# Context split once into fp16 parts, x2 written to a doubled buffer, and a new order of all engines, in a two-layer attention and expert kernel

## What is computed

```
x = x + autocorrelation(layernorm(x), ctx)     # per column: correlate over the 128 rows,
                                               # top 9 lags, softmax, sum of shifted ctx
x = x + experts0(layernorm(x))                 # xf @ W_base.T + b_base
                                               #   + top 2 of 8 experts, rank 16
x = x + window_attention(layernorm(x), ctx)    # rows are channels: q = Wq x, k = Wk ctx, v = Wv ctx,
                                               # 8 heads of 16, window of 16 columns, then Wo
x = x + experts1(layernorm(x))                 # top 2 of 4 experts, rank 16
```

## Time and profile before

| | us |
|---|---|
| median of three runs | 2023.16 (2018.21 to 2026.01) |
| profiled execution, its own time | 2025.97 |
| its span | 2024.1 |
| PE busy | 1855.6 (92%) |
| DVE busy | 1519.6 (75%) |
| ACT busy | 1347.2 (67%) |
| POOL busy | 1088.4 (54%) |
| mean granted clock of TensorE | 0.969 |

### The profile page before, as it was taken

The page is one execution under the profiler, slowest core; times in us unless marked ns, Lnnn a source line. Parts: engine busy times, 40 slices in busy tenths (PEclk is TensorE's granted clock), DMA queues, the critical chain, the costliest instruction groups (busy, mean ns, idle before and its releaser), DMA issues. The chain is left out here.

```text
span 2024.1 us, 49212 instructions
## 1 busy us (share of the span) xinstructions
PE 1855.6 (92%) x18912; PEld 1131.0 (56%) x18912; DVE 1519.6 (75%) x4529; ACT 1347.2 (67%) x1958; POOL 1088.4 (54%) x902
## 2 busy tenths in 40 slices
PE   4889999999999999999999999999999999999975
PEld 2355555665555655555565655566555565655543
DVE  6677777778777778777877777777777877877743
ACT  4267776677776677776667777667777666777652
POOL 2565555466555466555556655546655645655541
PEclk8899999999999999999999999999999999999985
DMA  5001110011111011111001111001111110111000
GB/s 217 22 33 53 52 52 31 31 52 41 52 52 36 27 50 41 52 52 52 31 31 43 50 52 52 31 31 49 45 52 52 44 39 31 41 52 42 21 6 17
DMA packets 25165, 91.56 MB, mean 45 GB/s; under 512 B 3184, under 2 KB 3312, under 8 KB 24624
## 3 DMA queue, kind: packets, MB, share of 16 engines
q1 hardware_dynamic: 25136, 91.17, 12.8%
HBM read 74.39 MB, written 16.78 MB: 45 GB/s over the span
## 5 line engine op out<-in xcount | busy, mean ns | idle before, releaser
L548 PE MATMUL pb<-w_base_h,even_words 128*128 128x512 f16 x1024 | 324.8, 379 | 0.4 <-ACT mid_t L851 0.4
L1370 POOL TENSOR_TENSOR p_hl<-sc,p_hl 128x512 f16<-128x512 f32 x128 | 178.1, 1391 | 180.3 <-ACT p_hl L730 180.3
L450 PE MATMUL pa<-ctx_a,tab 128*128 128x512 f32 x384 | 203.4, 655 | 35.6 <-ACT q_spec L730 24.3
L840 ACT ACTIVATE q_diag<-sc,par 32x1024 f32<-32x1024 f32 x192 | 216.1, 1141 | 19.9 <-DVE sc L1100 17.5
L1413 POOL TENSOR_TENSOR sc<-sc,sc_rec 128x512 f32<-128x512 f32 x128 | 134.2, 1048 | 146.8 <-DVE sc_rec L1176 146.8
L548 PE MATMUL pb<-w_base_l,even_words 128*128 128x512 f16 x512 | 193.9, 379 | 0.0
L617 PEld LDWEIGHTS pc<-sc_t,v_diag 128*128 128x128 f16 x6144 | 173.8, 97 | 32.9 <-issue 23.8
L450 PE MATMUL pa<-xn_a,tab 128*128 128x512 f32 x384 | 186.3, 609 | 1.5 <-ACT xn_a L730 1.5
L617 PE MATMUL pc<-sc_t,v_diag 128*128 128x32 f16 x6144 | 173.9, 177 | 6.5 <-ACT rows_c L730 6.5
L594 PE MATMUL pc<-k_h,q_diag 128*128 128x32 f16 x2048 | 169.1, 177 | 0.0
L595 PE MATMUL pc<-k_l,q_diag 128*128 128x32 f16 x2048 | 168.5, 177 | 0.0
(11 more groups left out here) (149 smaller groups left out, 5068.5 us busy)
## 6 DMA issues: line engine op xcount, KB each, us to landing
x_a<-in_x SPq DMA_DIRECT2D x32, 512.0 KB, 3.3
ctx_a<-in_ctx_in SPq DMA_DIRECT2D x32, 512.0 KB, 3.2
x_res<-in_x SPq DMA_DIRECT2D x32, 512.0 KB, 3.9
ctx_b<-in_ctx_in SPq DMA_DIRECT2D x32, 512.0 KB, 4.0
out<-rows_c SPq DMA_DIRECT2D x32, 512.0 KB, 2.9
v_diag<-in_base_w SPq DMA_DIRECT2D x4, 1024.0 KB, 10.1
tab<-in_spectra SPq DMA_DIRECT2D x1, 576.0 KB, 5.2
q_diag<-in_ra SPq DMA_DIRECT2D x1, 544.0 KB, 13.8
```

What stands on the lines that cost most here:

```text
L450: last = mm(place[:, n + h, :], lhsT, moving[:, h * HALF:(h + 1) * HALF], start=True, stop=True)
L548: mm(pb[:, h, :], rows[:, cols], weights[:, j, h * HALF:(h + 1) * HALF], start=(j == 0 and m == 0), stop=False)
L840: nc.scalar.activation(q_diag[rows, :, col:col + QB], source, ACT.Copy, scale=par[rows, a:a + 1]).then_inc(qd_out.sem, 1)
L1370: g_.tensor_tensor(part[:, :, :, LO], sc[:, g % 2, :, :], part[:, :, :, HI], ALU.subtract)\
```

## The change

1. **Context split once.** ctx is loaded once a batch (before: twice). ACT makes its high fp16 part (`ctx_high`), POOL the low one (`ctx_low`), in one of two slots of `ctx_hl`. The tables FWD, CTX_RE, CTX_IM and the weights Wk, Wv are split likewise at the start, and `project_ctx` makes each of the five context products from three fp16 products. ctx in float32 shares its buffer with `x_res`.
2. **Experts in fp16 parts.** The gates' result `mid` is split on DVE (two instructions more in `gates`), its transposes and the products in `b_base_end` and `c_delta` are fp16: six and four products of 128x512. `w_b0` and `w_b1` are split at the start.
3. **x2 straight to `x_c`**, which now has two slots; `b_move` on POOL is gone.
4. **Query product from PSUM.** `q_spec` and its copy are gone, DVE computes both c1 and c2 from `pa`. `a_values` is two copies of 64 rows and one of 128 (before: four of 64), with signs moved into the tables CORR_1 and CORR_2.
5. **Keys and values into `pa`**, before x2 is there (before: into `pb`, after x2).
6. `q_diag` is filled by halves of its blocks (twelve copies of 32x512 on ACT, four on POOL); the scores' first two groups need the first half only. `c_result` is in halves.
7. **All batches written out**, without a loop, in a new order on all engines. A step now begins in the middle of what was one: `live(k)` says whether batch i-k is there.

```diff
+            def project_ctx(n, slot, table):
+
+                high, low = ctx_hl[:, slot, 0, :], ctx_hl[:, slot, 1, :]
+                for h in range(2):
+                    cols = slice(h * HALF, (h + 1) * HALF)
+                    mm(pa[:, n + h, :], w_ctx_h[:, table, :], high[:, cols], start=True, stop=False)
+                    mm(pa[:, n + h, :], w_ctx_h[:, table, :], low[:, cols], start=False, stop=False)
+                    last = mm(pa[:, n + h, :], w_ctx_l[:, table, :], high[:, cols], start=False, stop=True)
+                return last
+
...
                 for h in range(2):
-                    last = mm(pb[:, h, :], mid_t[0][:, :], w_b0[:, h * HALF:(h + 1) * HALF],
-                              start=False, stop=True)
+                    cols = slice(h * HALF, (h + 1) * HALF)
+                    mm(pb[:, h, :], mid0_t[:, 0, :], w_b0_h[:, cols], start=False, stop=False)
+                    mm(pb[:, h, :], mid0_t[:, 0, :], w_b0_l[:, cols], start=False, stop=False)
+                    last = mm(pb[:, h, :], mid0_t[:, 1, :], w_b0_h[:, cols], start=False, stop=True)
                 last.then_inc(mm_ffn[0].sem, 1)
...
             def b_mid(b):
-                pe.wait_ge(mid_out[0].sem, mid_out[0].after(b))
-                nc.tensor.transpose(pb[:, 0, MID_AT:MID_AT + P], mid[0][:, :], ident[:, :])\
+                pe.wait_ge(midl_out[0].sem, midl_out[0].after(b))
+                nc.tensor.transpose(mid0_place[:, 0:P], mid_hl[0][:, 0, :], ident_h[:, :])
+                nc.tensor.transpose(mid0_place[:, P:2 * P], mid_hl[0][:, 1, :], ident_h[:, :])\
                     .then_inc(tr_mid[0].sem, 1)
...
-            def b_keys(b):
-                pe.wait_ge(ctxb_in.sem, ctxb_in.after(b))
-                pe.wait_ge(x2_out.sem, x2_out.after(b))
-                project(pb, 0, ctx_b, w_att[:, 1, :]).then_inc(mm_k.sem, 1)
-
-            def b_values(b):
+            def b_keys(b, slot):
+                if last_a(b):
+                    pe.wait_ge(prod_w.sem, prod_w.after(b))
+                else:
+                    pe.wait_ge(vagg_out.sem, vagg_out.after(b + 1))
+                project_ctx(2, slot, CTX_K).then_inc(mm_k.sem, 1)
+
+            def b_values(b, slot):
                 pe.wait_ge(kl_out.sem, kl_out.after(b))
-                project(pb, 0, ctx_b, w_att[:, 2, :]).then_inc(mm_v.sem, 1)
+                project_ctx(2, slot, CTX_V).then_inc(mm_v.sem, 1)
...
                 for h in range(2):
-                    last = mm(pc[:, h, :], mid_t[1][:, :], w_b1[:, h * HALF:(h + 1) * HALF],
-                              start=True, stop=True)
+                    cols = slice(h * HALF, (h + 1) * HALF)
+                    mm(pc[:, h, :], mid1_t[:, :], w_b1_hh[:, cols], start=True, stop=False)
+                    last = mm(pc[:, h, :], mid1_t[:, :], w_b1_l0[:, cols], start=False, stop=True)
                 last.then_inc(mm_ffn[1].sem, 1)
...
+            def step(i, odd, live):
+                if live(2):
+                    b_router(i - 2)
+                if live(3):
+                    c_attend(i - 3, 0)
+                if live(2):
+                    b_keys(i - 2, odd)
+                    b_base(i - 2, 1, 0)
+                if live(3):
+                    c_scores(i - 3, 3)
+                if live(2):
+                    b_base(i - 2, 1, 1)
+                    b_mid(i - 2)
+                if live(3):
+                    c_attend(i - 3, 1)
+                if live(2):
+                    b_values(i - 2, odd)
+                    b_base(i - 2, 0, 0)
+                if live(3):
+                    c_attend(i - 3, 2)
+                if live(2):
+                    b_base(i - 2, 0, 1)
+                if live(3):
+                    c_attend(i - 3, 3)
+                if live(2):
+                    b_base_end(i - 2)
+                if live(1):
+                    a_transpose(i - 1)
+                if live(3):
+                    c_output(i - 3)
+                if live(1):
+                    a_weights(i - 1, 1)
+                    a_weights(i - 1, 0)
+                if live(2):
+                    b_queries(i - 2)
+                if live(3):
+                    rows_to_features(i - 3, 1, 3, xn_c, pc)
+                    c_router(i - 3)
+                if live(1):
+                    a_aggregate(i - 1, 0)
+                    a_aggregate(i - 1, 1)
+                if live(3):
+                    c_mid(i - 3)
+                    c_delta(i - 3)
+                if live(0):
+                    a_context(i, odd)
+                if live(2):
+                    c_scores(i - 2, 0)
+                if live(0):
                     a_query(i)
-                if do_c:
-                    c_scores(c, 1)
-                if do_b:
...
+            def ctx_high(b, slot):
+
+                act.wait_ge(ctx_read.sem, ctx_read.after(b))
+                if not early(b):
+                    act.wait_ge(mm_k.sem, mm_k.after(b - 2))
+                    act.wait_ge(mm_v.sem, mm_v.after(b - 2))
+                copy(ctx_hl[:, slot, 0, :], ctx_f[:, :]).then_inc(ctxh_out.sem, 1)
+
+            def a_values(b):
+
+                act.wait_ge(mm_ctx.sem, mm_ctx.after(b))
+                if not first(b):
+                    act.wait_ge(sum_w.sem, sum_w.after(b - 1, 1))
+                for half in range(2):
+                    rows = slice(half * P // 2, (half + 1) * P // 2)
+                    other = slice((1 - half) * P // 2, (2 - half) * P // 2)
+                    copy(v_im[rows, :], pa_lo[other, :]).then_inc(v_out.sem, 1)
+                if not first(b):
+                    act.wait_ge(sum_w.sem, sum_w.after(b - 1))
+                copy(v_re[:, :], pa_lo).then_inc(v_out.sem, 1)
...
-                        act.wait_ge(mm_sc.sem, mm_sc.after(b - 1))
+                        act.wait_ge(mm_sc.sem, mm_sc.after(b - 1, 2 * half + 2))
                 rows = slice(32 * pair, 32 * pair + 32)
-                source = q_hl[rows, :].rearrange("p (n t) -> p n t", t=QB)
+                blocks = slice(half * NBLK // 2, (half + 1) * NBLK // 2)
+                source = q_hl[rows, :].rearrange("p (n t) -> p n t", t=QB)[:, blocks]
                 col = (2 * pair + a) * QB
-                nc.scalar.activation(q_diag[rows, :, col:col + QB], source, ACT.Copy,
+                nc.scalar.activation(q_diag[rows, blocks, col:col + QB], source, ACT.Copy,
                                      scale=par[rows, a:a + 1]).then_inc(qd_out.sem, 1)
 
...
             def a_product(b):
-                dve.wait_ge(q_out.sem, q_out.after(b))
+                if first(b):
+                    tables_ready()
+                dve.wait_ge(mm_q.sem, mm_q.after(b))
                 dve.wait_ge(v_out.sem, v_out.after(b, 2))
-                v.tensor_tensor(c1[:, :], q_spec[:, :], v_re[:, :], ALU.mult).then_inc(prod_q.sem, 1)
+                if not first(b):
+                    dve.wait_ge(mm_agg.sem, mm_agg.after(b - 1))
+                v.tensor_tensor(c2, pa_hi, v_im[:, :], ALU.mult).then_inc(prod_q2.sem, 1)
+                dve.wait_ge(v_out.sem, v_out.after(b))
...
+            def b_base(b, slot):
                 dve.wait_ge(mm_ffn[0].sem, mm_ffn[0].after(b))
                 dve.wait_ge(bias_added.sem, bias_added.after(b))
-                v.scalar_tensor_tensor(out=x_b[:, :], in0=pb_all, scalar=1.0 / W_SCALE, in1=x_b[:, :],
+                if not early(b):
+                    dve.wait_ge(x3_out.sem, x3_out.after(b - 2))
+                v.scalar_tensor_tensor(out=x_c[:, slot, :], in0=pb_all, scalar=1.0 / W_SCALE, in1=x_b[:, :],
                                        op0=ALU.mult, op1=ALU.add, accum_out=ln_sum[2][:, :])\
                     .then_inc(x2_out.sem, 1)
 
...
+                unscale = [SCALE0 / W_SCALE, SCALE1][n]
+                dve.wait_ge(mid_out[n].sem, mid_out[n].after(b))
+                v.tensor_scalar(mid_hl[n][:, 0, :], mid[n], unscale, None, ALU.mult)\
+                    .then_inc(midh_out[n].sem, 1)
+                dve.wait_ge(midh_out[n].sem, midh_out[n].after(b))
+                v.scalar_tensor_tensor(out=mid_hl[n][:, 1, :], in0=mid[n], scalar=unscale,
+                                       in1=mid_hl[n][:, 0, :], op0=ALU.mult, op1=ALU.subtract)\
+                    .then_inc(midl_out[n].sem, 1)
...
+            def c_result(b, h):
                 dve.wait_ge(mm_ffn[1].sem, mm_ffn[1].after(b))
-                v.tensor_tensor(rows_c[:, :], pc_all, rows_c[:, :], ALU.add).then_inc(x4_out.sem, 1)
+                cols = slice(h * HALF, (h + 1) * HALF)
+                v.scalar_tensor_tensor(out=rows_c[:, cols], in0=pc[:, h, :], scalar=1.0 / W_SCALE,
+                                       in1=rows_c[:, cols], op0=ALU.mult, op1=ALU.add).then_inc(x4_out.sem, 1)
...
-            def b_move(b):
-                pool.wait_ge(x2_out.sem, x2_out.after(b))
-                if not first(b):
-                    pool.wait_ge(x3_out.sem, x3_out.after(b - 1))
```

(30 more changed lines are left out.)

864 lines of the change are left out of this document (415 added, 449 removed).

## The result

| | before | after |
|---|---|---|
| median | 2022.96 (2018.21 to 2026.01) | 1871.71 (1870.98 to 1872.83) |
| ratio, 95% interval | | 0.9255 (0.9236 to 0.9274) |
| profiled execution: own time, span | 2025.97, 2024.1 | 1872.83, 1871.1 |
| PE, DVE, ACT, POOL busy | 92, 75, 67, 54% | 92, 84, 73, 55% |

What follows compares the result with a forecast made beforehand. PE fills the time, with DVE a second engine near the bound. Start 63, second turn 50, thirty turns of 55.4, low clock 10 and end 101.3 sum to 1886; plus 1.87, less 2.8: 1885 us, range 1832 to 1945.

Steps and rivals of the forecast that it cites:

- first residual: Start: a_residual of batch 0 moves from 57.5 to 63; DVE's weight splits cost 8.3, some 2.5 returns.
- second turn: Step from first to second a_residual, without c stage: 50 us, before 55.41.
- low clock: Turns where PE's clock falls to 0.50 after a thin stretch: 10 us in the run, as before.
- end: Batch 31 alone: 113.3 becomes 101.3; early keys and values 7 less, halves 3, c_delta at half clock 1.9.
- The walk: One turn followed along the new order from a_residual's end: DVE's waits sum to 5.0, added to its 50.4 gives 55.4.
- PE's savings: PE a turn: context products 2.4, b_base_end 0.4, c_delta 1.05, transposes of mid 0.2; work falls from 56.7 to 52.7.
- Tighter: Rival: stalls overlap, the turn falls towards PE's 52.7; at 53.5 and half the clock stretches, 1823 us; chance 0.11.
- "clock" rival: Thin stretches move around c_mid and features; a half-clock stretch every turn costs 53 instead of 10: 1928 us; chance 0.05.
- 2.5 that comes back: Start: some 2.5 us regained because w_ra0 on DVE no longer runs beside POOL's sums and delays them.
- ACT late: Rival: half q_diag copies at 0.79 instead of 0.63 lengthen the stretch before c_exp, 1.9 a turn: 1942 us; chance 0.11.
- Code: Written-out loop: taken as nothing; rival, 131 more instruction packets fully exposed cost 236 us, 2121; chance 0.03.
- The split saves nothing: Rival: waits keep PE idle, a turn stays 59.6 and only the end gains: 2010 us; chance 0.02.

Runs made afterwards that it cites:

- run 5: Changed kernel plus one idle DVE maximum over 1024 columns a turn, ahead of the two products of query and context: 1932.74 us.
- run 6: Changed kernel plus the same idle DVE maximum over 1024 columns, ahead of the last scores' maximum: 1871.14 us.
- run 7: Changed kernel plus the idle DVE instruction ahead of the products of query and context, and PE computes the second group of scores twice: 1901.56 us.
- run 8: Changed kernel; ACT waits for the last constants only ahead of step 2, POOL clears v_diag right after the sums of batch 0: 1862.0 us.
- run 4: Changed kernel with query blocks filled whole: six copies of 32x1024 on ACT in place of twelve of 32x512: 1927.91 us.
- run 3: Changed kernel with both fp16 splits undone, context products and experts in float32: 1974.45 us.
- run 2: Changed kernel with only the context products in float32 again: 1933.98 us.
- run 1: Kernel before with its five loops written out and nothing else: 2020.76 us, ratio 0.9997.
- the four reorderings: Changed kernel with ACT and POOL in other orders around the start of a turn, the last two with start edits: 1928.22, 1895.41, 1862.25, 1845.68 us.

## Why the prediction held, and where its terms were off

| term | forecast | measured |
|---|---|---|
| first residual | 63 | 66.4 |
| second turn | 50 | 54.05 |
| thirty turns | 30x55.4 = 1662 | 1649.2 |
| low clock | 10 | 0 |
| end | 101.3 | 101.5 |
| span | 1886 | 1871.1 |

The errors have two signs: first residual and second turn were put 7.5 too low, turns and clock 22.8 too high. That the first hide a third of the second is luck.

- **The turn** was forecast as 50.4 of DVE and 5.0 of its waits and is 49.5 and 5.5. PE's work, forecast 52.7, is 52.8. The walk named the waits well: 1.19 at the last scores (1.2 forecast), 0.57 ahead of x2 (0.8), 0.78 at the residual (1.0), 0.79 at the first sums (0.45), 0.69 at the first scores (0.5). The gate's exp was put at 0.7 and is 0.35. `rows_c` was expected among DVE's longest waits and is only 0.24. Not named: 0.39 for a root and 0.33 for the low part of the softmax. DVE's term was 0.9 too large: the split of the gates costs 1.0 (twice 0.29 and twice 0.22), not 1.2, and the three normalisations take 2.4 before and 2.2 now, because the next instruction starts 0.08 ahead of each one's end. The other half of the 0.9 isn't traced.
- **PE's savings.** 2.4 for the context and 1.65 for the experts were priced; undoing them one after the other gives 1.95 and 1.35 a turn. The size of a product was right (1.29); a fifth of the saving did not show in the turn. That DVE is "a second engine near the bound" depends on the place: in runs 5 and 6 1.2 us more on DVE cost 0.95 or more between the residual and c1, and nothing ahead of the last scores, where it waits 1.19 anyway. Other places were not tried. "Tighter" was the nearest rival by time; what it names, stalls that overlap down to PE's work, is not what happened: 2.2 us of waits remain.
- **Low clock** is the step that failed. "10 us for low-clock stretches as before" took them as a property of the kernel; the clock is full in all thirty turns. Before, in the six slow turns, they begin behind a wait of 0.79 for the `q_spec` copy, which the change removes:

```profile
542.85 1.97 PE L450 MATMUL pa<-ctx_a,tab 128*128 128x512 f32 x2 [0.79 <-ACT q_spec L730]
```

  That this wait is the cause before was argued from the row, not tried; that a wait of PE can be the cause is shown by runs 5 and 7. Its length alone doesn't decide: the same 0.79 stands in all the other turns before, at full clock, and the changed kernel waits 0.95 for `sc_t` in every turn without a drop. The "clock" rival had the mechanism, but the wait ahead of c1 came out at 0.51 only, and the clock stayed full.
- **The start** was put 3.4 too early by this trace; over the seven traces with the same start it is 0.1 to 4.3. The step "the first residual: 57.5 to 63" priced DVE's instructions and did not see that ACT's wait for all constants now stands ahead of a copy that needs none of them. Run 8 brings the residual 5.3 earlier. The "2.5 that comes back" was also too much: beside `w_ra0` POOL's second sum took 3.39 in place of the 2.36 that such a sum takes, so that about 1.0 could come back:

```profile
50.22 3.39 POOL L1363 TENSOR_TENSOR prob<-prob,v_re 128x1024 f32<-128x1024 f32 x1
```

- **The second turn**, 50, is 54.05: its price took no account of the 6.6 us for which POOL's clearing holds up L1049. The kernel before had the same kind of loss in that turn: its L1006 took 7.29 at 89.80, beside the clearing of `q_diag` on POOL (6.93 at 89.61). Run 8 gives back 6.5.
- **The end** has the right sum of wrong parts. Halves were priced at 3 and give 4.6 (run 4), the splits at 1.9 and give 6.0 (run 3: 107.5; the context 1.3 of it, 102.8 in run 2). If the parts add, early keys and values and the rest are left with 1.2 of the 11.8, not 7; that was not tried alone. Each is the difference of two traces, and the end is 102.5 in run 8, whose edits don't touch it, so 1 us of each can be chance, the context's 1.3 above all.
- **Query copies** take 0.717 each, in the middle between 0.63 (forecast) and 0.79 ("ACT late"). The chain through ACT was right in kind: run 4 shows what its late end costs.
- **Code.** Nothing for 131 more packets, as taken. By the Trainium skill ("Runtime: NRT & Kernel Launch", Instruction fetch mechanics) sequential fetch is mostly hidden; run 1 agrees. It also says that a taken branch can cost a fetch stall and that unrolling is preferred for it; here 0.9997 (0.9981 to 1.0014) shows no such gain.
- **The split saves nothing**, at 2010, is excluded: 1871.7, and 103 of the 151 us saved are from the two splits.

## What to carry to other kernels

Where the busiest engine has waits at few places of a turn, find the stretch behind its last wait: here four fifths of the work taken off it were paid. Work added to another engine cost most of its price where the busiest one waited for it, and nothing where that engine itself was waiting. Before moving an instruction, look at what the move puts beside it on the other engines, and at the buffer waits of whatever follows it: three of the four reorderings here lost their gain to a neighbour of what they moved. A whole wait for "all constants", or for both copies of a pair, is worth splitting when the first reader needs one of them.
